# Token-mixing product of a Trainium2 kernel as four 64x64 blocks, placed behind the own-token products

## What is computed

```python
x = x + _L0_cond_ref(x, ...)   # one of 16 experts for a sequence: x @ W[id] + b[id]
x = x + _L1_cond_ref(x, ...)   # shared projection plus a low-rank adapter
x = x + _L2_cond_ref(x, ...)   # attention over a window of 256 cached keys and the own ones, 8 heads, then Wo
x = x + _L3_cond_ref(x, ...)   # token mixing, below

def _L3_cond_ref(x, subjects, weights, bias):
    w = weights[subjects]                      # (64, 64) for each sequence
    b = bias[subjects]                         # (64,)
    out = jnp.einsum('bct,bcd->bdt', x, w)     # mixes the 64 tokens c into 64 tokens d
    out = out + b[:, :, None]
    return out
```

## Time and profile before

| | us |
|---|---|
| median of 3 runs | 1006.88 (1006.56 to 1006.94) |
| span of the profiled execution | 960.7 |
| difference of the two, outside the profiled span | 46.2 |
| phase two in the span, first scores to the end | 523 to 960.7 |
| a pair of steps of phase two (one even, one odd) | 13.27 |
| even step, odd step | 7.08, 6.19 |

### The profile page before, as it was taken

How to read it: one execution, slowest core, us unless ns; L and a number is a source line. 1 busy time by engine, 2 the same in 40 slices (tenths; PEclk the granted TensorE clock), 3 DMA queues, 4 the chain that set the end, 5 groups by cost and what they waited for, 6 DMA issues and landing times.

```text
span 960.7 us, 22134 instructions
## 1 busy us (share of the span) xinstructions
PE 931.3 (97%) x6253; PEld 687.7 (72%) x6253; DVE 604.0 (63%) x1788; ACT 383.8 (40%) x1061; POOL 512.8 (53%) x469
## 2 busy tenths in 40 slices
PE   6899999999999999999997899999999999999997
PEld 4566767667676666767666678877878788878785
DVE  5434344666565644346554777778777787777874
ACT  2121212212122121221223656666666666666662
POOL 1245454544536467664566666555666556565530
PEclk9999999999999999999999999999999999999999
DMA  9888887786776868777734666666666666666741
GB/s 300 272 279 289 292 299 233 262 279 229 257 244 235 279 215 272 233 240 277 265 131 140 192 197 179 192 211 179 201 193 184 211 215 191 197 191 204 220 124 46
DMA packets 105162, 212.48 MB, mean 221 GB/s; under 512 B 29563, under 2 KB 52056, under 8 KB 96930
## 3 DMA queue, kind: packets, MB, share of 16 engines
q1 hardware_dynamic: 71042, 145.54, 45.1%
q0 software_dynamic: 25088, 57.74, 20.5%
q10 hardware_dynamic: 8992, 8.73, 2.8%
HBM read 204.39 MB, written 33.86 MB: 248 GB/s over the span
## 4 chain that ended last, share of the span: by engine, by line
PE 91%; SPq 3%; DMA 2%; issue 1%; DVE 1%; ACT 1%; POOL 0%; DVEq 0%; POOLq 0%; ACTq 0%
PE banks L587 11%; PE banks L802 9%; PE banks L705 9%; PE banks L753 8%; PE banks L790 7%; PE banks L626 6%; PE banks L634 6%; PE banks L636 6%; PE banks L776 6%; PE banks L795 4%; PE banks L730 4%; PE banks L838 3%; PE banks L695 3%; PE banks L710 3%; PE banks L597 2%; PE banks L770 1%
## 5 line engine op out<-in xcount | busy, mean ns | idle before, releaser
L546 POOL DMA_INDIRECT ring<-new_rows,idx x128 | 129.4, 1011 | 82.2 <-DVE big L1278 55.5
L458 POOL TENSOR_TENSOR rms<-ss,neg_half 128x12 f32<-128x12 f32 x31 | 70.8, 2284 | 165.3 <-DVE ss L1184 165.3
L930 ACT ACTIVATE big<-big,neg_max 128x320 f32<-128x320 f32 x256 | 141.3, 555 | 4.2 <-DVE neg_max L1242 4.0
L1242 DVE CUSTOM_DVE_ANT_0 big<-banks,mask 128x320 f32<-128x320 f32 x256 | 114.6, 485 | 32.8 <-PE banks L753 30.7
L587 PE MATMUL banks<-ring 128*64 128x512 f32 x512 | 118.8, 607 | 2.0 <-DMA ring<-in_w 2.0
L871 ACT ACTIVATE x2t_hi<-banks 128x512 fp32r<-128x512 f32 x32 | 19.1, 598 | 235.5 <-PE banks L597 235.5
L920 ACT ACTIVATE kt<-banks 128x384 f32<-128x384 f32 x128 | 62.0, 485 | 95.6 <-PE banks L731 95.5
L587 PEld LDWEIGHTS banks<-ring 128*64 128x64 f32 x512 | 34.6, 138 | 81.6 <-issue 80.4
L535 POOL DMA_INDIRECT ring<-new_rows,idx x64 | 61.5, 961 | 53.2 <-PE banks L776 48.7
L753 PE MATMUL banks<-kt,q_in 64*128 64x128 f32 (+2 forms) x768 | 86.8, 358 | 1.3 <-ACT kt L920 1.3
L1278 DVE TENSOR_SCALAR big<-big,recip 128x320 f32<-128x320 f32 x256 | 86.0, 398 | 2.3
(11 more groups left out here) (169 smaller groups left out, 1980.8 us busy)
## 6 DMA issues: line engine op xcount, KB each, us to landing
ring<-in_w SPq DMA_DIRECT2D x62, 1024.0 KB, 6.0
ring<-in_xt SPq DMA_DIRECT2D x32, 256.0 KB, 2.7
x_in<-in_x SPq DMA_DIRECT2D x32, 256.0 KB, 5.4
bias_in<-in_b SPq DMA_DIRECT2D x64, 128.0 KB, 5.4
x_dram<-x SPq DMA_DIRECT2D x32, 256.0 KB, 5.0
q_dram<-q_t ACTq DMA_DIRECT2D x32, 256.0 KB, 2.3
new_rows<-kv_out SPq DMA_DIRECT2D x32, 256.0 KB, 4.8
q_in<-q_dram SPq DMA_DIRECT2D x64, 128.0 KB
```

Of the source, the lines that this page charges most:

```text
L546: pool.indirect_dma_start(out=kv[:, s, c, :], out_offset=None, in_=new_rows, in_offset=bass.IndirectOffsetOnAxis(ap=idx[:, b, 1 + c:2 + c] ...
L930: nc.scalar.activation(prob[:, s % 2, g * NK:(g + 1) * NK], sm[:, s % 2, g, :], ACT.Exp, bias=neg_max[:, s % 2, g:g + 1], scale=-1.0, accu ...
L1242: V.tensor_tensor_reduce(sm[:, s % 2, g, :], ps_s[g], mask[:, s % 2, k0:k0 + NK], 1.0, 3.0e38, ALU.add, ALU.min, accum_out=neg_max[:, s % ...
```

## The change

The own `bd` tile, the POOL instruction that cleared it and DVE's x4 instruction go. In their place:

- The mixing product becomes four products of 64 partitions by 64 columns of weights with 256 columns of x3 each: for column half i and sequence h, `w3` of sequence h (partitions 64h to 64h+63) by x3's column half i, into partitions 64i to 64i+63 of bank `ps_mix[h]`. So x4 lies with its column halves on the two partition halves and the two sequences side by side. The two banks are `ps[7]` (that of `ps_x`, as before) and `ps[5]`, which is also `ps_pt[1]`.
- `w3 = w3_in + eyes`, the identity added by DVE behind x3 in the even step, so that the residual x3 comes out of the product.
- The product stands behind `values()` in PE's step instead of ahead of it. PE's waits for x3 and w3 stay ahead of `values()`.
- ACT adds the bias and moves x4 out of the banks with two instructions at the start of the odd step. PE waits for these in the odd step ahead of `transpose_probs()`.
- SP loads each bias column twice (seven DMAs for a pair) and stores x4 with two DMAs instead of one. SP's wait for the cleared `bd` ahead of the mask loads becomes waits for the end of phase one on PE.
- ACT's loop writes out its first 8 steps instead of 4.

```diff
@@ PE
                 def transpose_probs():
 
                     pe.wait_ge(prob_ready, G * b)
+                    if s % 2 == 1 and on(b, 5, NB):
+                        pe.wait_ge(x4_ready, pair)
...
                 if second_half:
 
-                    pe.wait_ge(ld_pair[pair_s], PAIR_DMAS * 16 * (j * 2 + s // 4))
-                    for i, (n0, n1) in enumerate(COLUMN_PARTS if is_last(pair) else WHOLE):
-                        pe.wait_ge(x3_ready, pair + 1 + i)
-                        nc.tensor.matmul((ps_mix[i] if is_last(pair) else ps_x)[:, n0:n1], bd[:, pair_s, :], x3[:, pair_s, n0:n1],
-                                         start=True, stop=True).then_inc(l3_done, 1)
-                if on(b, 1, NB) and not behind_probs:
+                    pe.wait_ge(w3_ready, pair + 1)
+                    pe.wait_ge(x3_ready, pair + 1)
+                    if not behind_probs and on(b, 1, NB):
+                        values()
+                    if is_last(pair):
+                        pe.wait_ge(x4_ready, pair)
+                    for i, (n0, n1) in enumerate(COLUMN_PARTS):
+                        if i == 1 and is_last(pair):
+                            pe.wait_ge(x3_ready, pair + 2)
+                        for h in range(2):
+                            last = nc.tensor.matmul(ps_mix[h][T * i:T * i + T, :], w3[T * h:T * h + T, pair_s, :],
+                                                    x3[T * h:T * h + T, pair_s, n0:n1], start=True, stop=True, skip_group_check=True)
+                        if i == 1 or is_last(pair):
+                            last.then_inc(l3_done, 1)
+                elif on(b, 1, NB):
                     values()
@@ ACT, at the start of its step
+                if s % 2 == 1 and on(b, 5, NB):
+
+                    pair, pair_s = (b // 2 if isinstance(b, int) else j * 2 + s // 2) - 2, s // 2
+                    wait(act, st_out[pair_s], 2 * 16 * (j - 1))
+                    act.wait_ge(ld_pair[pair_s], PAIR_DMAS * 16 * j)
+                    for i in range(2 if is_last(pair) else 1):
+                        rows = slice(T * i, T * i + T) if is_last(pair) else slice(0, P)
+                        act.wait_ge(l3_done, pair + 1 + i)
+                        for h in range(2):
+                            last = nc.scalar.activation(x4[rows, pair_s, D // 2 * h:D // 2 * (h + 1)], ps_mix[h][rows, :], ACT.Identity,
+                                                        bias=sbias[rows, pair_s, h:h + 1])
+                        last.then_inc(x4_ready, 1)
                 if on(b, -1, NB):
                     copy_keys(b + 1, s + 1, 0)
@@ DVE
-                if finished:
-
-                    wait(dve, st_out[pair_s], 16 * (j - 1))
-                    for i, (n0, n1) in enumerate(COLUMN_PARTS if is_last(pair) else WHOLE):
-                        dve.wait_ge(l3_done, pair + 1 + i)
-                        dve.wait_ge(x3_ready, pair + 1 + i)
-                        V.scalar_tensor_tensor(x4[:, pair_s, n0:n1], (ps_mix[i] if is_last(pair) else ps_x)[:, n0:n1], sbias[:, pair_s, 0:1],
-                                               x3[:, pair_s, n0:n1], ALU.add, ALU.add).then_inc(x4_ready, 1)
...
+                    wait(dve, l3_done, pair - 1)
+                    V.tensor_tensor(w3[:, pair_s, :], w3_in[:, pair_s, :], eyes[:, :], ALU.add).then_inc(w3_ready, 1)
```

More of the change, by code:

```diff
@@ L76, in build @@
         ident = sb("ident", [P, P])
+        eyes = sb("eyes", [P, T])
         iota = sb("iota", [P, WIN])
@@ L168, in build @@
         x2_in, x3, x4 = x_in, bias_in, x1
-        bd = sb("bd", [P, 2, P])
-        sbias = sb("sbias", [P, 2, 1])
+        w3 = sb("w3", [P, 2, T])
+        sbias = sb("sbias", [P, 2, 2])
+        w3_in = sb("w3_in", [P, 2, T])
         banks = ctx.enter_context(nc.psum_tensor("banks", [P, 8 * BANK], F32))
@@ L392, in phase_two @@
                     k, t = (b // 2 if isinstance(b, int) else j * 2 + s // 2) - 3, 1 - s // 2
-                    for i, (n0, n1) in enumerate(COLUMN_PARTS if is_last(k) else WHOLE):
-                        sp.wait_ge(x4_ready, k + 1 + i)
-                        sp.dma_start(a["out"][bass.ds(k, 1), :, n0:n1].rearrange("o p d -> (o p) d"), x4[:, t, n0:n1]).then_inc(st_out[t], 16)
+                    for i, (n0, n1) in enumerate(COLUMN_PARTS):
+                        if i == 0 or is_last(k):
+                            sp.wait_ge(x4_ready, k + 1 + i)
+                        sp.dma_start(a["out"][bass.ds(k, 1), :, n0:n1].rearrange("o (h c) n -> c (o h) n", h=2),
+                                     x4[T * i:T * i + T, t, :].rearrange("c (h n) -> c h n", h=2)).then_inc(st_out[t], 16)
                 if s % 2 == 0 and on(b, 2, NB):
@@ L968, in phase_two @@
                                          ps_o[:, 0:2 * P].rearrange("p (c t) -> p c t", c=2 * GP), ACT.Copy).then_inc(othi_ready, 1)
-            loop(act, phase_two, 4, 4, NB + 1, NB - 4)
+            loop(act, phase_two, 4, 8, NB + 4, NB - 4)
         @block.vector
@@ L1210, in make_mask @@
                                 ALU.is_lt, ALU.mult).then_inc(mask_ready, 1)
+            for h in range(2):
+                link(V.tensor_copy(eyes[T * h:T * h + T, :], ident[T * h:T * h + T, T * h:T * h + T]))
             dve.wait_ge(wo_hi_ready, 1)
@@ L1231, in split_outputs @@
                                     ot_hi[:, t, :, T * h:T * h + T].bitcast(F32), ALU.subtract).then_inc(ot_ready, 1)
-                added, finished = s % 2 == 0 and on(b, 4, NB), s % 2 == 1 and on(b, 5, NB)
+                added = s % 2 == 0 and on(b, 4, NB)
                 pair, pair_s = (b // 2 if isinstance(b, int) else j * 2 + s // 2) - 2, s // 2
@@ L1283, in phase_two @@
                     split_outputs()
-            loop(dve, phase_two, 4, 8, NB + 4, NB - 4)
+            loop(dve, phase_two, 4, 8, NB + 3, NB - 4)
 def kernel(x, itok_B_0_15, itok_B_0_6, itok_Bx257_0_4111, itok_B_37_3939, itok_B_0_7, fside_8xS_0, L0_cond_W, L0_cond_b,
```

22 lines of the change are left out of this document (11 added, 11 removed).

## The result

| | before | after |
|---|---|---|
| median, us | 1006.74 (1006.56 to 1006.94, 4 runs) | 1023.69 (1020.00 to 1033.41, 4 runs) |
| ratio | | 1.0183 [1.0149, 1.0217] |
| span of the profiled execution | 960.7 | 1021.2, of a run of 1022.97 |

The change costs 17 us by the medians, and between 15 and 22 us by the interval of the ratio. 13.8 us were forecast, and the time is inside the range. How these microseconds come about is another matter, and most of what follows is on that.

The account below looks back on a forecast made before the run. In even steps PE and ACT were taken as tied, so the removed product becomes a wait; 30 even steps x 0.45 = 13.5 us, the end +0.3: +13.8, span 974.5 plus 46.2 outside gives 1020.7 us, range 1017 to 1034.

Parts of the forecast that it names:

- main term: Mixing product standing uncovered behind the values in even steps: 30 x 0.45 us, 13.5 us slower.
- The tie of PE and ACT, and the cover that turns into a wait: Even steps, ahead of the values: ACT's copy sets their start, so the product's 0.88 us become PE waiting, not saving.
- The four corners at once, 0.45 us: Mixing product on PE: all four 64x64 blocks run at once, 0.43 us plus 0.02 us for getting four started.
- The rival of two at a time: Mixing product: only two blocks run side by side, 0.86 to 0.90 us net, +26.9 us, 1033.8 us; chance 0.12.
- the strict order: Mixing product: each next block starts only with the previous one's second half, 1.08 us, 1039.9 us; chance 0.03.
- Its net time is added to each even step: Product behind the values delays the next scores, on which the odd step hangs: 0.45 us in each of 30 steps.
- ACT's two additions: Start of odd step: 0.63 us, ending about 0.8 us in, covered before PE's wait at 1.66 us; no cost.
- w3's sum: DVE's added 128x64 addition in the even step: 0.15 us, ahead of its copy of probabilities, costing nothing in the loop.
- SP's added DMAs: Three more DMAs a pair, some 1.4 us of issuing in 13.3, issued a pair ahead; cost nothing.
- The end, +0.3 us: Last pairs: w3's sum +0.15, shorter product -0.56, last pair's longer tail with ACT's four instructions +0.75; sum +0.3 us.
- PE's lower clock, left out: PE falling to its lower clock in the new wait ahead of the values; chance under 0.01, no time added.
- The 46.2 us outside the span: Time taken to lie outside the profiled span, added to the forecast span of 974.5 us to give 1020.7.

Follow-up runs that it names:

- e2: Changed kernel with the waits ahead of the values reordered: outputs' low part, third copy, DVE's copy, ACT's copy; ratio 1.0159 to the kernel before.
- e3: Changed kernel with ACT doing three exponentials instead of four ahead of its two copies in even steps; ratio 1.0143 to the kernel before.
- e10: Kernel before with ACT's copy of the second transposed block made twice in even steps, so the values start later; ratio 1.0024.
- e7: Changed kernel with the four-corner product ahead of the values, bank 0 for the second sequence, and the bias additions by DVE; ratio 1.0170 to the kernel before.
- e1: Kernel before with the mixing product, in its old block-diagonal form, moved behind the values in even steps; ratio 1.0026.
- e8: Kernel before with PE's mixing product left out, DVE's last sum reading x3 in its place; ratio 0.9990.
- e9: Changed kernel with its four-corner product left out, ACT's additions reading x3 in its place; ratio 1.0159 to the kernel before.
- e4: Changed kernel with each pair's bias loads taken out, the first two experts' bias loaded once ahead of the loop; ratio 1.0155 to the kernel before.
- e6: Kernel before with each pair's two bias loads made three times, two of the copies unused; ratio 1.0013.

## Why the prediction came out right, and where it was wrong

**The number is right, its main term is not, and that the two agree is luck**: the 13.5 us of the main term are not there, and other terms, put at nothing or at 0.3 us, come to about as much. By the steps of the prediction:

- *The tie of PE and ACT, and the cover that turns into a wait*: seen as forecast in the pair shown (ACT's copy ends 5.37 us into the step, PE idle for 1.07 us ahead of the values), but for the time of a pair it doesn't count: an even step shortened or lengthened ahead of the values (e2, e3, e10) changes the pair by 0.1 us at most. The 0.09 us behind the copy came out as 0.36: wait instructions are worked off there one by one, which the product had covered.
- *The four corners at once, 0.45 us*: 0.43 measured. The rival of two at a time falls. So does the strict order as the prediction reckoned it, with both records of a product together: the first records of all four start within 0.02 us, the second ones 0.24 to 0.27 us later (e7). The argument for the lower figure had one reading wrong: the products of scores (64 rows by 128 columns) share the columns of the array, only the own-token products share nothing. Under "TensorEngine Tiling (Array Packing)", "Tiling Modes", the Trainium skill says that tiles operate independently, and the trace agrees: L850's first record starts at 664.42, inside L800's.
- *"Its net time is added to each even step", 13.5 us*: this step failed. It holds for the even step (7.94 us by the median instead of 7.32) and not for the pair (14.71 instead of 14.54), since the odd step begins with a lateness that shrinks for it (6.80 instead of 7.21). Three runs say so: the product moved (e1, +2.6 us in all, though a product of 1.06 us now stands right ahead of the odd step's scores), left out of the kernel before (e8, nothing) and out of the changed one (e9, nothing).
- *ACT's two additions, "covered with a full microsecond to spare"*: this failed too, and costs. They take 0.83 us rather than 0.63, and behind a release 1.1 us into the odd step they end at 2.2 us, past the transposes' 1.66 and, what counts here, past DVE's low part of the outputs, which ends at 667.11, 1.95 us into the step. The part of the pair behind the release grows from 5.54 to 5.76 us, 0.22 x 31 = 7 us. The prediction had named the point ("it would hurt at once if the copy came over 0.7 us later") and given it no chance. The kernels compared differ in more than the additions, but the timelines place all of the 0.22 us between the release and the transposes, and e7, without them on ACT, is at 5.54 again.
- *w3's sum*: 0.21 instead of 0.15 us, off the path in the loop. *SP's added DMAs*: nothing that e4 and e6 can show.
- *The end, +0.3 us*: +2.0. From the last scores to the end of the span it is 23.2 us (998.0 to 1021.2), before 21.2 in both profiles. ACT's four additions take 1.68 us for an estimated 1.15, and from the last x3 to their end it is 2.65 us (1015.58 to 1018.23) where 2.0 were forecast. Each of the last stores takes 0.60 us to issue where it took 0.33, and the last bytes land 2.04 us behind the last sum instead of 1.36.

```profile
1015.50 0.21 DVE L1290 TENSOR_TENSOR w<-w_in,eyes 128x64 f32<-128x64 f32 x1
```
```profile
1016.55 1.68 ACT L967 ACTIVATE x<-banks,sbias 64x256 f32<-64x256 f32 x4 [4.05 <-PE banks L850]
```

- *PE's lower clock, left out*: this term had been put at nothing, and it isn't. Between the scores of steps 4 and 63, the six profiles of before and its variants have one or two windows in which half the clock is granted; the six of the changed kernel with the additions on ACT have two to seven. A pair that holds one lasts 1.2 to 4.7 us longer than the median; two of these pairs are longer without a window too, by 1.3 to 2.4 us. In sum these pairs add some 5 us in the profiles of before and 10 in those of the changed kernel. By the whole runs, the mean granted clock is 0.985 in 27 runs of the changed kernel and its variants e2, e3, e4 and e7, and 0.991 in 55 of the kernel before. In these 55 a clock lower by 0.01 goes with 5.5 us more within one chip and session (1 to 8 us from one session to another), so by this estimate the 0.006 are worth some 3 us. That PE's new waits bring the windows is likely and not shown.
- *The 46.2 us outside the span*: an error of reading that did no harm to the sum and hid everything above. A median 46 us from the profile's span was the sign that the profile was of another kind of execution.

What the runs bear out is then 6 to 7 us behind the release (14.74 against 14.54 us for the median pair is 6), 2 at the end and 3 to 5 with the clock: 11 to 14 of the 15 to 18. A sum that needs no such split agrees: from the scores of step 4 to those of step 60, 28 pairs, it is 409 to 416 us in the six profiles of before and its variants (mean 413.3) and 422 to 429 in the six with the additions on ACT (mean 424.8). These are 11.4 us, and 13.4 with the end. The remaining few I can't place; they are within what the runs scatter.

**What stays open** is what holds PE's completions. Excluded are the bias loads (e4 to e6) and the amount of PE's work ahead (e8). The release keeps a nearly fixed distance to the third gather of the even step, 1.7 to 1.9 us by the medians of thirteen profiles of twelve kernels (within one, a standard deviation of 0.06 to 0.26). But PE's transposes of probabilities in the same step, to which the gathers themselves are tied, are as good a mark: the release comes 5.8 to 6.1 us behind their start, with a deviation of 0.08 to 0.29. So the profiles do not tell a hold by the gathers from one by PE's own course. And now and then the distance to the gather is 0.9 to 1.0 us, as in steps 60 and 61 of the kernel before profiled again. In the first profile of before that gather stands at the same place and holds nothing, so it can't be the whole cause:

```profile
740.56 1.00 POOL L546 DMA_INDIRECT ring<-new_rows,idx  x1 [0.30 <-issue]
```

(step from 733.38; ACT's copy at 740.58). Moving the gathers wasn't tried. It is what I would try next, since a pair without the lateness is 1.3 us shorter. That the forecast's main term would hold in an execution such as the first profiled one is likely and not shown.

## What to carry to other kernels

Before trusting a profile for a sum, hold its span against the timed runs: where they differ by more than a few us, profile the kernel again and see which repeated wait is new. A cost "added to each step" is only shown when the step after doesn't give it back, so count over the whole period of the loop; taking the operation out altogether tests this in one run. And an operation with slack against one arrival should be priced against the latest arrival of that producer, above all if an engine's queue waits for it.

## What was new about the hardware

- Completions of TensorE can reach the waiting engines 1.5 us and more after the records' ends, several at once, in one execution and not in another of the same kernel (ACT's copy 1.67 us into the odd step, at 747.75, against 0.12 us, at 740.58).
- Four 64x64 corners with fp32 operands run at once: eight records of 256 columns in 0.66 us from first start to last end (e7), 0.43 us net (after).
- Wait instructions whose conditions are already met cost PE 0.11 us each when nothing is streaming (values 0.36 us behind the copy in after, 0.14 in e2); behind a running product they cost nothing (0.09 in the first profile of before).
- An addition of 128x256 with a bias column takes ScalarE 0.47 us (L967 of after), a copy of that size 0.37 (L956).
